# Cross-attention layer: attention scores in 32-row tiles and one fp32 pass over the values

## The reference

```python
def attention(q, k, v, mask):
    scores = jnp.einsum('bhqd,bhkd->bhqk', q, k) / jnp.sqrt(jnp.float32(HD))
    scores = scores * mask - 10000.0 * (1.0 - mask)
    probs = jax.nn.softmax(scores, axis=-1)
    return jnp.einsum('bhqk,bhkd->bhqd', probs, v)
ln_out = layernorm(hidden_states, ln1_s, ln1_b)
q, k, v = jnp.split(ln_out @ w_qkv + b_qkv, 3, axis=-1)
x = hidden_states + merge_heads(attention(..., ltor_mask)) @ w_ao + b_ao
ln_out = layernorm(x, ln2_s, ln2_b)
q = ln_out @ w_q + b_q
k, v = jnp.split(encoder_states @ w_kv + b_kv, 2, axis=-1)
x = x + merge_heads(attention(..., cross_mask)) @ w_co + b_co
return x + gelu(layernorm(x, ln3_s, ln3_b) @ w1 + b1) @ w2 + b2
```

## Time and profile before

| | |
|---|---|
| three timed runs | 2080.98, 2083.93, 2086.44 us (median 2083.93) |
| span of the profiled execution | 2081.6 us |
| PE busy | 1957.9 us, 94% of the span |
| DVE, ACT, POOL busy | 1390.2, 1072.6, 884.1 us (67%, 52%, 42%) |
| attention stage | about 0 to 1347 us |
| MLP stage | about 1347 us to the end |

### The profile page before, as it was taken

One profiled execution on the slowest core, in us unless ns is written; L12 is line 12 of the kernel. 1 busy time (PEld: TensorE's weight loads), 2 busy tenths in 40 slices (PEclk: granted clock), 3 DMA queues, 4 the chain that ended last, 5 costly groups with the idle time before them and its releaser, 6 DMA issues. The chain is left out here.

```text
span 2081.6 us, 39412 instructions
## 1 busy us (share of the span) xinstructions
PE 1957.9 (94%) x12304; PEld 1657.1 (80%) x12304; DVE 1390.2 (67%) x2571; ACT 1072.6 (52%) x2562; POOL 884.1 (42%) x910
## 2 busy tenths in 40 slices
PE   5999999999998999999999999699999999999999
PEld 5788888888787778887887887588888888888887
DVE  6889889888888998899889888662322323232221
ACT  4666666667667666666676666443222222222222
POOL 5556556556557655555565555450201012020110
PEclk9999999999999999999999999899999999999999
DMA  6332222222223432332232224501010101101010
GB/s 172 94 91 70 65 77 68 66 72 74 61 73 88 106 97 73 86 93 72 77 96 71 73 83 104 165 28 51 11 55 5 60 12 48 50 10 54 6 41 21
DMA packets 144820, 141.51 MB, mean 68 GB/s; under 512 B 20736, under 2 KB 94464, under 8 KB 144768
## 3 DMA queue, kind: packets, MB, share of 16 engines
q1 hardware_dynamic: 144768, 140.85, 24.2%
HBM read 82.07 MB, written 25.17 MB: 52 GB/s over the span
## 5 line engine op out<-in xcount | busy, mean ns | idle before, releaser
L1046 POOL TENSOR_TENSOR a_t_s<-a_t_s,a_m_add 128x512 f32<-128x512 f32 x256 | 345.4, 1349 | 334.3 <-DVE a_t_s L837 334.1
L1315 DVE TENSOR_TENSOR m_g_r<-m_g_t,m_g_r 128x512 fp32r<-128x512 f32 x128 | 95.9, 750 | 476.1 <-ACT m_g_r L1294 476.0
L1223 PE MATMUL m_ps_h<-k_bd,wt 128*128 128x512 f32 x1536 | 378.7, 397 | 2.9 <-PEq L360 2.9
L1223 PEld LDWEIGHTS m_ps_h<-k_bd,wt 128*128 128x128 f32 x1536 | 289.2, 189 | 72.4 <-issue 3.3
L1237 PE MATMUL m_ps_y<-m_down_hi,m_g_r 128*128 128x512 f32 x1024 | 343.8, 396 | 0.1
L704 ACT ACTIVATE a_p_s<-a_t_s,a_nb 128x128 f32<-128x128 f32 x1024 | 328.3, 391 | 8.3
L524 PE MATMUL a_ps_c<-a_xT,wt 128*128 128x256 f32 x2304 | 318.2, 288 | 11.6 <-DVE a_xT L885 5.5
L524 PEld LDWEIGHTS a_ps_c<-a_xT,wt 128*128 128x128 f32 x2304 | 285.4, 191 | 25.3 <-issue 10.9
L1237 PEld LDWEIGHTS m_ps_y<-m_down_hi,m_g_r 128*128 128x128 f32 x1024 | 192.4, 188 | 45.1 <-issue 0.5
L1278 ACT ACTIVATE m_g_t<-m_ps_h,bias_cols 128x512 f32<-128x512 f32 x128 | 88.1, 688 | 270.9 <-PE m_ps_h L1223 270.7
L688 ACT CAST a_pT<-a_ps_t 128x512 f16<-128x512 f32 x256 | 150.0, 586 | 150.7 <-PE a_ps_t L502 150.4
(11 more groups left out here) (85 smaller groups left out, 3210.9 us busy)
## 6 DMA issues: line engine op xcount, KB each, us to landing
k_bd<-a_k_r SPq DMA_DIRECT2D x512, 64.0 KB, 2.1
a_x_t<-in_x SPq DMA_DIRECT2D x32, 256.0 KB, 2.8
a_res_t<-in_x SPq DMA_DIRECT2D x32, 256.0 KB, 2.8
x_after_self<-a_y_t SPq DMA_DIRECT2D x32, 256.0 KB, 2.0
a_x_t<-x_after_self SPq DMA_DIRECT2D x32, 256.0 KB, 2.7
a_enc_t<-in_ctx SPq DMA_DIRECT2D x32, 256.0 KB, 2.9
raw_wt<-in_w SPq DMA_DIRECT2D x32, 256.0 KB, 4.7
a_res_t<-x_after_self SPq DMA_DIRECT2D x32, 256.0 KB, 3.9
```

The costliest lines, as they stand in the source:

```text
L1046: nc.gpsimd.tensor_tensor(t_s[:, n % 2], t_s[:, n % 2], m_add[:, b].unsqueeze(1).to_broadcast([P, HQ, P]), ALU.add).then_inc(s["biased"], 1)
L1223: last = nc.tensor.matmul(ps_h[j % 2][:], w1[hw][:, j // KC, kc, (j % KC) * P:(j % KC + 1) * P], xT[:, hx, kc], start=(k == 0), stop=(k == ...
```

## The change

Queries and keys of all sixteen heads are projected first, one `keys(g + 1, c)` and one `queries(g + 1, c)` in each of slots 4 to 7 of the group ahead, into a buffer that holds both (`qk`, with `q_t` and `k_t`). A sequence's scores are then computed at once, for all sixteen heads (`scores(g, b)`, at the ends of slots 7 and 3): 48 products of 32 rows (one head's 32 channels) and 128 columns, with four heads in the four 32-row tiles of the array, into four PSUM banks. There is no block-diagonal buffer and there are no DMAs that fill it. A slot is now four heads of sequence 0 (slots 0 to 3) or of sequence 1 (slots 4 to 7).

The exponential subtracts the maximum without the lift and writes the row sums (`accum_out`); DVE inverts them and multiplies the probabilities (`normalise`) before they are turned. `copy_probs` copies the turned probabilities once, as fp32, and `weigh_values` multiplies fp32 values (32 columns a head, as the stationary operand) by them: four products of 128 columns a slot, whose result is already the turned context. So `low_probs`, `context`, `flip_ctx`, the value pieces (`value_top`, `value_middle` on ACT, `value_rest`, `value_last` on POOL) are gone, and `high_context` and `low_context` split what `ps_o` holds. `flip_x` and `flip_enc` share `ps_c` with the projections, in slots 2 and 3. The splits of weights and some loads move to other slots, and the loop over groups is one shorter, with one more group written out.

```diff
                     def scores(g, n):
-                        pe.wait_ge(kbd_in[i], at(g * (16 * HQ * KC // 2) + 16 * HQ * (c // 2 + 1)))
-                        for x, (hq, hk) in enumerate(PASSES):
-                            last = nc.tensor.matmul(ps_s[n % 2][:], q_r[:, i, hq, b * P:(b + 1) * P],
-                                                    k_bd[:, i, hk, b], start=(x == 0), stop=(x == 2))
+                    def scores(g, b):
+                        pe.wait_ge(s["k_copied"], at((g + 1) * KC))
+                        pe.wait_ge(s["q_copied"], at((g + 1) * KC))
+                        if b > 0 or known(g, 1):
+                            pe.wait_ge(s["masked"], at((g * GB + b) * KC))
+                        for c in range(KC):
+                            for x, (hq, hk) in enumerate(PASSES):
+                                for j in range(HQ):
+                                    r = slice(HD * j, HD * (j + 1))
+                                    last = nc.tensor.matmul(ps_s[:, j, c], q_t[r, hq, c, cols], k_t[r, hk, c, cols],
+                                                            start=(x == 0), stop=(x == 2))
...
                     def weigh_values(g, n):
                         for j in range(HQ):
-                            for h in (HI, LO):
-                                last = nc.tensor.matmul(ps_o[:, j, 0:VW], pT[:, n % 2, h, j * P:(j + 1) * P],
-                                                        v_b[:, b, HQ * c + j, 0:VW], start=(h == HI), stop=(h == LO))
+                            h = HQ * c + j
+                            last = nc.tensor.matmul(ps_o[HD * j:HD * (j + 1), c], v_t[:, b, HD * h:HD * (h + 1)],
+                                                    pT[:, n % 2, j], start=True, stop=True)
...
                     def keys(g, c):
                         if c > 0 or known(g, 1):
-                            pe.wait_ge(s["ql_done"], at(g * KC + c))
+                            pe.wait_ge(s["q_copied"], at(g * KC + c))
                     def queries(g, c):
-                        pe.wait_ge(s["kl_done"], at(g * KC + c + 1))
+                        pe.wait_ge(s["k_copied"], at(g * KC + c + 1))
...
                     def flip_enc(g, b):
                         pe.wait_ge(enc_in[b], at(16 * (g - NG + 1)))
+                        pe.wait_ge(s["xTl_done"], at(g * GB + b + 1))
...
                     def exponent(g, n):
-                        nc.scalar.activation(nb[:, n % 2], mx[:, n % 2], ACT.Identity, bias=lift_t[:],
-                                             scale=-1.0).then_inc(s["nb_done"], 1)
                         for j in range(HQ):
                             last = nc.scalar.activation(p_s[:, n % 2, j], t_s[:, n % 2, j], ACT.Exp,
-                                                        bias=nb[:, n % 2, j:j + 1])
+                                                        bias=mx[:, n % 2, j:j + 1],
+                                                        accum_out=sums[:, n % 2, j:j + 1])
...
+                    def invert_sums(g, n):
+                        nc.vector.reciprocal(rcp[:, n % 2], sums[:, n % 2]).then_inc(s["inverted"], 1)
+
+                    def normalise(g, n):
+                        dve.wait_ge(s["inverted"], at(slot_no(g, n)))
+                        nc.vector.tensor_tensor(p_s[:, n % 2], p_s[:, n % 2],
+                                                rcp[:, n % 2].unsqueeze(2).to_broadcast([P, HQ, P]),
+                                                ALU.mult).then_inc(s["normal"], 1)
...
                     def slot(g, n, cur, prev, nxt):
                         ahead = norms_next(g, cur, nxt)
+                        if n == 2 and ahead:
+                            norm(g + 1, 1)
                         if cur if n >= 1 else prev:
                             maxima(*lag(g, n, 1))
                         if cur:
                             mask_scores(g, n)
+                        if n == 0 and ahead:
+                            statistics(g + 1, 0)
+                            statistics(g + 1, 1)
+                        if cur if n >= 2 else prev:
+                            invert_sums(*lag(g, n, 2))
...
+                        if cur if n >= 2 else prev:
+                            normalise(*lag(g, n, 2))
+                        if n >= 4 and nxt and (cur or prev):
+                            low_cols(g + 1, n - 4, WK, k_t, "kh_done", "k_copied")
...
+                        if n == 1 and ahead:
+                            centre(g + 1, 0)
+                            norm(g + 1, 0)
+                            centre(g + 1, 1)
+                        if n == 2 and prev:
+                            low_context(g - 1, 1)
+                        if n == 6 and cur:
+                            low_context(g, 0)
...
+                        if n in (2, 3) and nxt:
+                            flip_x(g + 1, n - 2)
+                            if crosses(g + 1):
+                                flip_enc(g + 1, n - 2)
```

More of the change, by code:

```diff
@@ L323, in run @@
             def run(engine, slot):
-                for n in range(4, NS):
+                for n in range(2, NS):
                     slot(-1, n, False, False, True)
@@ L342, in run @@
                         slot(g, n, True, True, True)
+                for n in range(NS):
+                    slot(gN - 2, n, True, True, True)
                 for n in range(NS):
@@ new lines, in slot @@
+                        if n in (1, 2) and cur:
+                            values(g, n - 1, 0)
+                        if n >= 4 and nxt:
+                            keys(g + 1, n - 4)
+                        if n in (0, 1):
+                            if n == 0 and prev:
+                                outputs(g - 1, 0, 1, cur)
+                            if n == 1 and cur:
+                                values(g, 0, 1)
+                        if cur if n >= 3 else prev:
+                            weigh_values(*lag(g, n, 3))
@@ L632, in slot @@
+                        if n == 2 and cur:
+                            values(g, 1, 1)
+                        if n == 3 and prev:
+                            outputs(g - 1, 1, 1, cur)
+                        if n >= 4 and nxt:
+                            queries(g + 1, n - 4)
                         if cur if n >= 2 else prev:
                             transpose_probs(*lag(g, n, 2))
-                        if n == 5 and nxt:
-                            (flip_enc if crosses(g + 1) else flip_x)(g + 1, 1)
@@ L646, in slot @@
-                        if n == 7 and nxt:
-                            keys(g + 1, 1)
-                        if n == 4 and nxt:
-                            (flip_enc if crosses(g + 1) else flip_x)(g + 1, 0)
-                        if n in (3, 4, 5, 6) and prev:
-                            outputs(g - 1, (n - 3) // 2, (n - 3) % 2, cur)
-                        if n == 7 and nxt:
-                            values(g + 1, 0, 0)
-                        if n in (0, 1, 2) and cur:
-                            values(g, (n + 1) // 2, (n + 1) % 2)
@@ L664, in slot @@
+                        if n == 3 and cur:
+                            scores(g, 1)
+                        if n == 7 and nxt:
+                            scores(g + 1, 0)
                         if n in (0, 1, 4, 5) and leads(g):
@@ L757, in high_flip @@
                             act.wait_ge(s[name], at(value))
-                        nc.scalar.copy(dst_t, ps_x[:]).then_inc(s[high], 1)
+                        nc.scalar.copy(dst_t, ps_c[:]).then_inc(s[high], 1)
                     def flip_x(g, b):
@@ L802, in slot @@
-                        if n == 4 and nxt:
-                            (flip_enc if crosses(g + 1) else flip_x)(g + 1, 0)
-                        if not (cur or prev):
+                        if n in (0, 3) and prev:
+                            output_row(g - 1, n // 3)
+                        if n in (1, 2) and cur:
+                            copy_values(g, n - 1)
+                        if n >= 4 and nxt:
+                            copy_cols(g + 1, n - 4, WQ, q_t, "q_done", "qh_done")
@@ L813, in slot @@
+                        if not (cur or prev) and n >= 4:
+                            split_weights(g, n)
                         if n in (0, 1, 4, 5) and leads(g):
@@ L943, in slot @@
-                        if n == 5 and nxt:
-                            (flip_enc if crosses(g + 1) else flip_x)(g + 1, 1)
-                        if n == 6 and nxt and crosses(g + 1):
-                            flip_x(g + 1, 1)
-                        if cur if n >= 3 else prev:
-                            context(*lag(g, n, 3), (g + 1) * GB + n if n in (1, 2) and ahead else None)
+                            invert_sums(*lag(g, n, 2))
+                        if n == 0 and ahead:
+                            dve.wait_ge(s["stats_done"], at((g + 1) * GB + 2))
@@ L975, in slot @@
```

(2 more changed lines are left out.)

458 lines of the change are left out of this document (159 added, 299 removed).

## The result

| | before | after |
|---|---|---|
| median of four runs | 2084.84 us | 2460.69 us (2457.92 to 2463.16) |
| ratio | | 1.1805, 95% interval 1.1788 to 1.1822 |
| span of the profiled execution | 2081.6 us | 2458.3 us |
| first scores | 29.9 us | 45.3 us |
| first product of the MLP | 1346.7 us | 1722.3 us |

The change costs 376 us, all of it ahead of the MLP (1722.3 - 1346.7 = 375.6). Predicted were 2540 us with a range of 2260 to 2860: the sign and the mechanism held, the size was 79 us too large.

What follows compares the result with a forecast made beforehand. Waits, not TensorE's work, were to decide: groups of 52.3 us in self-attention and 56.4 in cross-attention, against 39.3 and 40.7, sixteen each, add 459 us to 2081.6, giving 2540 us; range 2260 to 2860.

Steps and rivals of the forecast that it cites:

- The ring: Slots 4 to 7: keys and queries follow each other through the one bank `ps_c`, DVE late; 6.4 us a slot.
- The row sums: Writing them on ACT with the exponentials: between nothing and 0.30 us each, 0.2 taken.
- S: Time of one batch of 48 score products on PE: 2.9 us, between bounds of 1.6 and 5.5.
- PE's own work: Per group, 11.4 us added against 9.3 removed, so TensorE loses about 2 us.
- V: One slot's four fp32 products of values with probabilities on PE: 0.7 us, from 0.5 to 1.15.
- The chain of slots 0 to 3: Scores, mask, `normalise` and DVE alternating with POOL; PE waits 2.6 us in slot 2; second scores end at 27.1 us.
- Cross-attention: `flip_enc` waits in slots 2 and 3 for `flip_x`'s low part: twice 2.05 us, group 56.4 instead of 52.3.
- The startup: Eight ring halves instead of three before the first scores: some 20 us more, cancelled by a last group without ring.
- tiles go one after another: Rival: score products in the row tiles do not overlap, S = 5.5 us, 5.2 a group more, 2706 us; chance 0.15.
- The clock rival: PE's clock stays at 1.2 GHz in the rings of slots 4 to 7: 10 us a group more, 2860 us; chance 0.12.
- The first rival: `normalise` on DVE goes free of POOL: 8.3 us a group less, 2275 us; chance 0.13.
- The faster rival: TensorE stays the bound, its work falls 2.1 us a group with no longer waits: 2015 us; chance 0.03.

Runs made afterwards that it cites:

- Two banks: The changed kernel with the queries' projections in the idle bank `ps_r` instead of `ps_c` in slots 4 to 7: 2211.24 us.
- `normalise` moved: The changed kernel with inversion and `normalise` ahead of the mask on DVE, in slot 0 the statistics too: 2367.05 us, ratio to before 1.1362.
- the runs in one, two and four tiles: The changed kernel with all 48 products of a batch in the first row tile, 2930.82 us, or first two, 2585.50; four is the changed kernel, 2460.69.
- the last version: The changed kernel with `normalise` first, two banks, POOL's work and `norm` moved, context and keys copied before exponentials, `flip_enc` away from `flip_x`: 1981.34 us, 0.9517 of before.

## Why the prediction was right, step by step

**The ring** was predicted at 6.4 us a slot and took 6.21. From the start of the maxima at 327.31: add_bias until 2.66, in the trace 329.95 - 327.31 = 2.64; `normalise` until 3.2, in the trace 330.49 - 327.31 = 3.18; queries at 3.8, in the trace 3.63. The row sums were mis-sized: four exponentials with their reads took 329.58 - 328.02 = 1.56, where 1.28 and 0.8 more had been set. Two banks show that the ring was the main cause; `normalise` moved shows that its collision added 0.3 of the slot.

**S** was the worst term: 2.9 predicted, 1.56 measured, just under the lower bound of 1.6. Twice a group that is 2.7 us, most of the 3.4 by which the period was missed: self-attention took (438.24 - 291.45) / 3 = 48.9 from first scores to first scores, instead of 52.3 and a little under the 50 to 58 that were to show the prediction right. I took a value between the bounds because "four tiles use four banks", which no row supported; the runs in one, two and four tiles show that the lower bound was the mechanism, four at a time with 0.11 us for each product in its tile.

**PE's own work** was said to lose 2 us a group. That was wrong in sign: 2 x 1.56 + 8 x 0.36 (a V's start to the next start) = 6.0 replace 9.3, a gain of 3.3. The conclusion that the waits decide held all the same; in the last version, without the waits, the gain is there (35.9 a group against 39.3).

**The chain of slots 0 to 3**: second scores were to end at 27.1 and ended at 24.8 (363.34 + 1.56 - 340.09): the two shorter S take off 2.7, and the wait of slot 2 gave 0.5 of it back, 3.08 for 2.6. **Cross-attention** was to take 4.1 more than self-attention; it took (1607.75 - 1171.21) / 8 = 54.6, so 5.7 more. The timeline of PE in the group at 1171 us:

```profile
1189.64 1.09 PE L546 MATMUL a_ps_c<-ident,a_enc_t 128*128 128x128 f32 x4 [1.65 <-DVE a_xT L764]
...
1198.65 0.63 PE L546 MATMUL a_ps_c<-ident,a_enc_t 128*128 128x128 f32 x4 [1.49 <-DVE a_xT L764]
```

From the start of `flip_x`, whose transposes take 0.60, to that of `flip_enc` it is 0.60 + 1.65 = 2.25 and 0.60 + 1.49 = 2.09, 4.3 for the 4.1 forecast. The sum had left out the time of `flip_enc` itself on PE, and the row product behind the first wait ran at a clock of 0.50 (1189 to 1195 us): to the next transposes it took 5.7 us, and 4.9 in self-attention at 308 us. **The startup** was 15.5 us later for 20, and the end, without a ring, gave about as much back: 16 x (48.9 - 39.3) + 16 x (54.6 - 40.7) = 376, the whole loss.

**Rivals.** That tiles go one after another was refuted by S = 1.56 us. The clock rival was half right: the clock does fall, but by the trace's record of the granted clock 171 of the 229 us at the lower level lie in slots 0 to 3, and only 27 in slots 4 to 7. The first rival, `normalise` free, did not happen, and its price was too high as well. Of its 8.3 a group 4.8 stood for slots 4 to 7, 2 and 3, which is 154 of the 266 us; the run that freed `normalise` alone, and left the alternation, gained 94. The step that failed there is that slots 4 to 7 would take 5.7: my own working had ACT's copy ready at 3.3, later than `normalise` at 3.2, so ACT stood next in line and no slot could drop by 0.7. The faster rival was excluded by "eight gaps of 1.09", which was right for one bank only: with a second bank and POOL out of the way the gaps close, at 2038 us, and at 1981 once `flip_enc` no longer waits behind `flip_x`.

The lower clock accounts for more than the 35 us by which PE's busy time rose. By the trace's record of the granted clock PE was busy for 184 us at the lower level, and for 21 before. Twelve products take 2.93 us there and 1.65 at the full clock, so, taking work there as twice as long, half of the difference, 82 us, is an estimate of what the lower clock added; PE's smaller work offsets the rest. The versions with shorter waits in slot 2 have the higher clock (0.953 after, 0.972 with `normalise` first, 0.991 in the last). Not settled is what the lower clock costs of the whole time, since PE waits behind that work anyway: no run held the waits and changed the clock alone.

## What to carry to other kernels

Before a projection is given a second place in a slot, count what stands between two uses of its bank: product, copy, low part and two handoffs are one ring, and short products cannot cover it; an idle bank in the same slots was worth more here than any step of reordering (249 us against 104 at most). When a stall is taken away, read from the same timeline what was next in line, since that is the gain. A DVE instruction with both operands in SBUF belongs where POOL is idle: ahead of the instruction that releases POOL, not behind it (698 against 1414 ns here).

## What the hardware showed that I had not expected

- 48 products of 32 rows and 128 columns took 1.56 us in four row tiles, 0.027 us each, 0.056 in two and 0.111 in one; three in a row written for the same tile cost nothing (1.59).
- In one tile the granted clock fell from 1.00 to 0.50 within a batch in which PE was busy without a gap; in four tiles 59 of the 64 batches took 1.56 us, the one at 363.34 at a clock of 1.00.
- The read of a row sum is a record of its own on ACT, 187 ns on average, and yet the exponentials follow each other every 0.39 us with it, against (1.28 - 0.39) / 3 = 0.30 in the earlier trace rows without.
- The collision goes both ways: POOL's instructions of 1.28 us took 1.55 to 1.73 between DVE's.
